# Gated cross attention and six layers on one core: the norm between them placed inside the last turns and the first pass

## What is computed

```python
x = x + jnp.tanh(g_xattn[0]) * _L0_xattn_ref(_layernorm(x), ctx_1024, ctx_1024, ...)
x = x + jnp.tanh(g_ffn[0]) * _L0_ffn_ref(_layernorm(x), ...)
# _L0_ffn_ref:
for i in range(6):
    x = attn_layer(shift_tokens(x), ...) + x
    x = ffn_layer(shift_tokens(x), ...) + x
```

## Time and profile before

| | us |
|---|---|
| median of 3 runs | 1986.11 (1985.73 to 1987.90) |
| profiled execution, its time | 1993.02 |
| its span | 1991.2 |
| PE busy | 1858.3 (93% of the span) |
| DVE busy | 1589.7 (80%) |
| ACT busy | 1045.7 (53%) |
| POOL busy | 903.9 (45%) |
| cross attention, up to the last `x1` update | 0 to 266.3 |
| the norm between, up to the first projection | 266.3 to 290.1 |

### The profile page before, as it was taken

The page is one execution under the profiler, slowest core; times in us unless marked ns, Lnnn a source line. Parts: engine busy times, 40 slices in busy tenths (PEclk is TensorE's granted clock), DMA queues, the critical chain, the costliest instruction groups (busy, mean ns, idle before and its releaser), DMA issues.

```text
span 1991.2 us, 84866 instructions
## 1 busy us (share of the span) xinstructions
PE 1858.3 (93%) x35408; PEld 1303.1 (65%) x35408; DVE 1589.7 (80%) x3092; ACT 1045.7 (53%) x1879; POOL 903.9 (45%) x1231
## 2 busy tenths in 40 slices
PE   6888858899999999999999999999999999999996
PEld 3444424676767777777767677776767676777674
DVE  5565557788988888888888888888889888888883
ACT  2444423455555656555555556565556555465553
POOL 1000015364554646464555546464645555464640
PEclk7898888999999999999999999999999999999997
DMA  2001006556566656566565666565665646564650
GB/s 69 10 7 64 0 3 100 83 80 102 74 122 109 94 82 94 117 95 108 78 104 72 122 109 94 82 93 117 93 110 76 106 71 124 104 95 83 91 91 22
DMA packets 73332, 166.87 MB, mean 84 GB/s; under 512 B 16592, under 2 KB 23504, under 8 KB 72400
## 3 DMA queue, kind: packets, MB, share of 16 engines
q0 software_dynamic: 36864, 100.71, 37.9%
q1 hardware_dynamic: 36432, 65.68, 12.7%
HBM read 20.57 MB, written 1.05 MB: 11 GB/s over the span
## 4 chain that ended last, share of the span: by engine, by line
PE 69%; DVE 9%; issue 7%; DMA 2%; ACT 0%; DVEq 0%; POOL 0%; POOLq 0%; ACTq 0%
PE ps L997 14%; PE ps L1033 8%; PE ps L1087 7%; PE ps L1107 6%; PE ps L1057 6%; PE ps L1141 5%; PE ps L1009 5%; PE ps L1070 4%; PE ps L1100 3%; DVE big L815 3%; PE ps L1131 3%; PE ps L1021 3%; DVE big L825 2%; DMA big<-big 2%; PE ps L1048 2%
## 5 line engine op out<-in xcount | busy, mean ns | idle before, releaser
L477 POOL DMA_DIRECT2D big<-big x768 | 607.0, 1497 | 62.4 <-DVE big L807 43.9
L564 ACT ACTIVATE big<-ps 128x512 f32<-128x512 f32 x384 | 228.4, 595 | 587.6 <-PE ps L997 540.0
L997 PE MATMUL ps<-big,wn_sb 128*128 128x256 f32 x1536 | 411.2, 396 | 17.5 <-issue 14.9
L815 DVE TENSOR_TENSOR big<-big,ps 128x512 f32<-128x512 f32 x384 | 249.6, 680 | 93.2 <-PE ps L1021 82.8
L997 PEld LDWEIGHTS ps<-big,wn_sb 128*128 128x128 f32 x1536 | 275.4, 192 | 69.6 <-issue 16.5
L468 POOL TENSOR_TENSOR big<-big 128x512 f32<-128x512 f32 x96 | 123.4, 1285 | 360.8 <-ACT big L581 360.8
L804 DVE TENSOR_TENSOR big<-ps,tab 128x512 f32<-128x512 f32 x384 | 262.0, 682 | 11.0 <-ACT big L564 10.9
L807 DVE TENSOR_TENSOR big<-ps,tab 128x512 f32<-128x512 f32 x384 | 259.0, 674 | 0.0
L1141 PE MATMUL ps<-big,wo_sb 128*128 128x256 f32 x768 | 214.5, 382 | 0.0
L443 POOL COPY big<-xs 64x256 f32 x144 | 79.2, 550 | 263.5 <-DVE xs L843 257.6
L1033 PE MATMUL ps<-wn_sb,big 128*64 128x512 f32 x768 | 182.0, 611 | 0.7 <-DVE big L807 0.7
(11 more groups left out here) (146 smaller groups left out, 2917.1 us busy)
## 6 DMA issues: line engine op xcount, KB each, us to landing
big<-big POOLq DMA_DIRECT2D x768, 128.0 KB, 5.0
big<-big SPq DMA_DIRECT2D x96, 256.0 KB
big<-big SPq DMA_DIRECT2D x96, 192.0 KB
wn_sb<-in_wn SPq DMA_DIRECT2D x6, 1024.0 KB, 10.0
wn_sb<-in_wn SPq DMA_DIRECT2D x6, 512.0 KB, 6.1
wo_sb<-in_wo SPq DMA_DIRECT2D x6, 512.0 KB, 4.0
w_sb<-in_w SPq DMA_DIRECT2D x6, 341.0 KB, 3.0
w_sb<-in_w SPq DMA_DIRECT2D x6, 192.0 KB, 3.3
```

The lines of the kernel that those rows point to most:

```text
L477: eng.dma_start(rot[to:to + 32, at:at + 4, :], src[32 * r:32 * r + 32], accum_op=ALU.add).then_inc(added[i], 16)
L564: eng.activation(sq[:, two, :], ps[:, i % 2, :].rearrange("p (a t) -> p a t", a=2), ACT.Square).then_inc(sq_d, 1)
L815: eng.tensor_tensor(hat[:, two, :], rot[:, two, :], ps[:, i % 2, :].rearrange("p (a t) -> p a t", a=2), ALU.mult).then_inc(hat_d, 1)
L997: mm = eng.matmul(ps[:, k % 2, a * T:a * T + T], wn_sb[:, u * P:u * P + P], sT, start=True, stop=True)
```

## The change

The norm of chunks 0, 1 and 2 (batches 0 to 5) is done inside turn 8, in the banks 0 and 1. Chunk 3 (batches 6 and 7, whose `x1` is complete only after turn 9) is centred and gets its variance, Ln and Exp behind turn 9, in the banks 4 and 5; its Newton step and product are put on DVE inside pass 0, behind `n`. PE makes the centred x directly, with the matrix `center` (identity minus mean), so the subtraction on DVE goes; Ln takes eps as its bias and the Newton step reads the variance from PSUM with + EPS in the same instruction, so the addition of eps goes. The scratch is three slots in a part of `big` that the cross attention doesn't use. POOL's zeroing moves ahead of its waits, and POOL and PE begin the layers with `nxn` at 3. The diff, cut to its core:

```diff
@@ -167,11 +167,8 @@
-        xc0 = view(CH * CW, CH, CW)
-        sq0 = view(CH * CW, CH, CW)
-        va0 = view(CH * CW, CH, CW)
-        z0 = view(CH * CW, CH, CW)
-        z1 = view(CH * CW, CH, CW)
+        used[0] = 22784
+        sq0, z0, z1 = (view(3 * CW, 3, CW) for _ in range(3))
         assert used[0] <= BIG
@@ -239,8 +236,10 @@
-        nmean, nxc, nsq, nvar, nva, nln, ny, nxn, nt = (
-            sem(n) for n in ("nmean", "nxc", "nsq", "nvar", "nva", "nln", "ny", "nxn", "nt"))
+
+        LN_BANKS = [(0, 1), (0, 1), (0, 1), (4, 5)]
+        nmean, nsq, nvar, nln, ny, nxn, nt = (
+            sem(n) for n in ("nmean", "nsq", "nvar", "nln", "ny", "nxn", "nt"))
@@ -428,13 +427,13 @@
             cross(eng, cross_body)
-            eng.wait_ge(nxn, CH)
-
...
             eng.wait_ge(zero, 7)
+            eng.wait_ge(xres, B + FREE)
+            eng.wait_ge(nxn, CH - 1)
@@ -485,7 +484,18 @@
+            def norm_squares(c):
+                eng.wait_ge(nmean, c + 1)
+                eng.activation(sq0[:, c % 3, :], ps[:, LN_BANKS[c][0], :], ACT.Square).then_inc(nsq, 1)
+
+            def norm_roots(c):
+                eng.wait_ge(nvar, c + 1)
+                eng.activation(z0[:, c % 3, :], ps[:, LN_BANKS[c][1], :], ACT.Ln, bias=part["eps"]).then_inc(nln, 1)
+                eng.wait_ge(nln, c + 1)
+                eng.activation(z0[:, c % 3, :], z0[:, c % 3, :], ACT.Exp, scale=-0.5).then_inc(ny, 1)
+
             def cross_body(b, X1, X2, X3):
+                late = X2 and not X1
                 def exps(first, last):
@@ -502,6 +512,8 @@
                     exps(0, 2)
+                if late:
+                    norm_squares(0)
                 if X1:
@@ -509,6 +521,8 @@
                     exps(2, 4)
+                if late:
+                    norm_roots(0)
                 if X1:
@@ -523,15 +537,24 @@
                     exps(6, 8)
+                if late:
+                    norm_squares(1)
                 masked(0)
...
                     exps(8, 10)
+                if late:
+                    norm_roots(1)
                 masked(1)
...
                     exps(10, 12)
+                if late:
+                    norm_squares(2)
                 masked(2)
...
                     exps(12, 14)
+                if late:
+                    norm_roots(2)
+                if X2:
                     eng.wait_ge(xsc, b * H)
@@ -544,15 +567,8 @@
-            for c in range(CH):
-                eng.wait_ge(nxc, c + 1)
-                eng.activation(sq0[:, c, :], xc0[:, c, :], ACT.Square).then_inc(nsq, 1)
-            for c in range(CH):
-                eng.wait_ge(nva, c + 1)
-                eng.activation(z0[:, c, :], va0[:, c, :], ACT.Ln).then_inc(nln, 1)
-            for c in range(CH):
-                eng.wait_ge(nln, c + 1)
-                eng.activation(z0[:, c, :], z0[:, c, :], ACT.Exp, scale=-0.5).then_inc(ny, 1)
+            norm_squares(CH - 1)
+            norm_roots(CH - 1)
@@ -622,6 +638,17 @@
+            def norm_rows(c):
+                eng.wait_ge(ny, c + 1)
+                eng.scalar_tensor_tensor(z1[:, c % 3, :], z0[:, c % 3, :], -0.5, z0[:, c % 3, :], ALU.mult, ALU.mult).then_inc(nt, 1)
+                eng.wait_ge(nt, 3 * c + 1)
+                eng.scalar_tensor_tensor(z1[:, c % 3, :], ps[:, LN_BANKS[c][1], :], EPS, z1[:, c % 3, :], ALU.add, ALU.mult).then_inc(nt, 1)
+                eng.wait_ge(nt, 3 * c + 2)
+                eng.scalar_tensor_tensor(z1[:, c % 3, :], z1[:, c % 3, :], 1.5, z0[:, c % 3, :], ALU.add, ALU.mult).then_inc(nt, 1)
+                eng.wait_ge(nt, 3 * c + 3)
+                eng.tensor_tensor(xs[:, 2 * c:2 * c + 2, 1:T + 1], ps[:, LN_BANKS[c][0], :].rearrange("p (a t) -> p a t", a=2),
+                                  z1[:, c % 3, :].rearrange("p (a t) -> p a t", a=2), ALU.mult).then_inc(nxn, 1)
+
@@ -668,6 +695,9 @@
                     eng.tensor_tensor(x1b, x1b, xproj, ALU.add).then_inc(xres, 1)
+                if X2 and not X1:
+                    for c in range(CH - 1):
+                        norm_rows(c)
                 if X1:
@@ -691,27 +721,6 @@
-
-            for c in range(CH):
-                eng.wait_ge(nmean, c + 1)
-                eng.tensor_tensor(xc0[:, c, :], x1[:, 2 * c:2 * c + 2, :].rearrange("p a t -> p (a t)"), ps[:, c, :],
-                                  ALU.subtract).then_inc(nxc, 1)
-            for c in range(CH):
-                eng.wait_ge(nvar, c + 1)
-                eng.tensor_scalar(va0[:, c, :], ps[:, 4 + c, :], EPS, None, ALU.add).then_inc(nva, 1)
-            for c in range(CH):
-                eng.wait_ge(ny, c + 1)
-                eng.tensor_tensor(z1[:, c, :], z0[:, c, :], z0[:, c, :], ALU.mult).then_inc(nt, 1)
-            for c in range(CH):
-                eng.wait_ge(nt, c + 1)
-                eng.scalar_tensor_tensor(z1[:, c, :], z1[:, c, :], -0.5, va0[:, c, :], ALU.mult, ALU.mult).then_inc(nt, 1)
-            for c in range(CH):
-                eng.wait_ge(nt, CH + c + 1)
-                eng.scalar_tensor_tensor(z1[:, c, :], z1[:, c, :], 1.5, z0[:, c, :], ALU.add, ALU.mult).then_inc(nt, 1)
-            for c in range(CH):
-                eng.wait_ge(nt, 2 * CH + c + 1)
-                eng.tensor_tensor(xs[:, 2 * c:2 * c + 2, 1:T + 1], xc0[:, c, :].rearrange("p (a t) -> p a t", a=2),
-                                  z1[:, c, :].rearrange("p (a t) -> p a t", a=2), ALU.mult).then_inc(nxn, 1)
@@ -790,6 +799,8 @@
                         eng.tensor_scalar(n_s, ps[:, 2, 0:T], 1e-24, 65536.0, ALU.max, ALU.mult).then_inc(ss_d, 1)
+                        if not Bh:
+                            norm_rows(CH - 1)
                     if kind == "N":
@@ -856,6 +867,17 @@
+            def center(c):
+                eng.wait_ge(xres, 2 * c + 2 + FREE)
+                if 0 < c < CH - 1:
+                    eng.wait_ge(nxn, c)
+                eng.matmul(ps[:, LN_BANKS[c][0], :], part["center"], x1[:, 2 * c:2 * c + 2, :].rearrange("p a t -> p (a t)"),
+                           start=True, stop=True).then_inc(nmean, 1)
+
+            def variance(c):
+                eng.wait_ge(nsq, c + 1)
+                eng.matmul(ps[:, LN_BANKS[c][1], :], mean_w, sq0[:, c % 3, :], start=True, stop=True).then_inc(nvar, 1)
+
@@ -939,14 +961,20 @@
                     tokens()
+                late = X2 and not X1
                 if X2:
                     scores(0)
+                if late:
+                    center(0)
+                if X2:
                     scores(1)
...
                     normed_tokens()
+                if late:
+                    variance(0)
                 if X2:
@@ -961,6 +989,10 @@
                         step(*which)
+                    if late:
+                        for at, do, c in ((0, center, 1), (2, variance, 1), (4, center, 2), (6, variance, 2)):
+                            if at == n:
+                                do(c)
                 if X2:
@@ -974,14 +1006,9 @@
             eng.wait_ge(xres, B + FREE)
-            for c in range(CH):
-                eng.matmul(ps[:, c, :], mean_w, x1[:, 2 * c:2 * c + 2, :].rearrange("p a t -> p (a t)"),
-                           start=True, stop=True).then_inc(nmean, 1)
-            for c in range(CH):
-                eng.wait_ge(nsq, c + 1)
-                eng.matmul(ps[:, 4 + c, :], mean_w, sq0[:, c, :], start=True, stop=True).then_inc(nvar, 1)
-            eng.wait_ge(nxn, CH)
-
+            center(CH - 1)
+            variance(CH - 1)
+            eng.wait_ge(nxn, CH - 1)
```

## The result

The changed kernel takes 1982.39 us, the median of 20 executions (1977.11 to 1993.87); the kernel before, over 20 executions beside it, 1990.02 (1985.73 to 1994.21). The ratio is 0.9964, 95% interval 0.9953 to 0.9975; applied to 1990.02 that is 7.2 us less, between 5.0 and 9.4. The forecast was 9.1 less and 1977.0, range 1972.5 to 1981.5: the sign is right, the size a little too large, and the time lies outside the range. Of the 5.4 us between 1977.0 and 1982.39, 3.9 are the kernel before itself: the three executions from which I counted had a median of 1986.11, the twenty 1990.02.

A forecast was written before the change was run, and what follows sets the result against it. PE, busy 93% of the span, was taken as the bound, with gains only where it stands still. -19.1 + 5.6 + 1.5 + 2.9 = -9.1, from 1986.1 to 1977.0 us, range 1972.5 to 1981.5.

The forecast's parts named there:

- Behind turn 9: From the last x1 update to the first projection: 4.65 us instead of 23.8, so -19.1 us.
- Turn 8, the walk: PE's order in turn 8 with six matmuls put in, including a 2.95 us stall before center(2): +5.6 us.
- `center(0)` falls into the 0.88: nothing: In turn 8, center(0) (0.86 us) fits PE's 0.88 us wait for DVE ahead of the output projection, at no cost.
- The clock: In turn 8, one stretch of about 3.4 us at half clock behind the stall: +1.5 us, ends 0 and +3.4.
- rival E: Turn 8 falls to half clock as a whole: slower by 3.4 us, up to +10 if pass 0 follows; chance 0.04.
- Pass 0: norm_rows(3) between n and c7, d7 delays m3, the values and the heads' norm: +2.9 us.
- The alternative that I named and didn't take: In pass 0, if m3's DMAs were held up by those of m2 rather than their own issue: about +1 us.
- Against the median: Whole kernel: -9.1 carried from the profiled execution to the median of the runs shown, 1986.1 - 9.1 = 1977.0 us.
- B: Clock stays up in turn 8, m3's DMAs hide 2 us in pass 0: -12.6, from -10.5 to -14; chance 0.17.
- C: Two half-clock stretches in turn 8, one over V1 to V3 in pass 0: -5.2, from -7.5 to -4; chance 0.18.
- A: The forecast: turn 8 loses about 7, behind turn 9 wins 19, pass 0 pays 3: -9.1, -7.5 to -10.5; chance 0.53.
- D: Turn 8 pays the whole serial chain of three chunks, 18.3 us: sum about +2, from -4 to +4; chance 0.08.

The follow-up runs named there:

- scores_paired: The changed kernel with center(0) behind scores(1) instead of between scores(0) and scores(1); ratio to the kernel before 0.9943, turns 8 and 9 35.34 us.
- clock_kept: The changed kernel with six extra matmuls of 256 columns, results unread, in the pause ahead of center(2); ratio to the kernel before 0.9947, turns 8 and 9 31.41 us.
- rows3_ahead: The changed kernel with norm_rows(3), DVE's four instructions for the last chunk, ahead of pass 0, behind the tables; ratio to the kernel before 0.9954, turns 8 and 9 31.25 us.
- all_behind: The change's norm, but chunks 0 to 2 behind turn 9 instead of in turn 8, each in its own banks; ratio to the kernel before 0.9990.
- rows3_split: The changed kernel with norm_rows(3) cut in two, first half ahead of pass 0, second ahead of c4; ratio to the kernel before 0.9946, pass 0 26.96 us.
- change_longer: The changed kernel with six extra matmuls of 256 columns in turn 9, during the division; ratio to the kernel before 0.9934.

## Why the prediction was right or wrong

*Behind turn 9* (-19.1): right, -19.3. Centre, square and variance at half clock took 4.51 us where I had 4.65; POOL's shift, the tables and the roots were ready, as said.

*Turn 8, the walk* (+5.6): the mechanism was right, the size too small. That `center(2)` waits for DVE's `xs` of the chunk before, that PE's `weigh` and ACT's exps are queued behind it, and that it is the only such wait: all in the trace, at 2.82 us for 2.95. Wrong was "`center(0)` falls into the 0.88: nothing". L973 began 3.86 us after the first scores instead of 2.80. I had priced a matmul by its own rate, 0.86, from a row of eight equal ones; between others one costs 1.05 (240.06 to 241.11), and it parted two `scores` that run into each other when they are neighbours; scores_paired puts that at 0.7. With 0.2 more for `center(1)` over its 0.84 of cover, the walk should have said 6.9 (31.2 us for turns 8 and 9); clock_kept and rows3_ahead, both at full clock, show 7.1 and 6.95.

*The clock* (+1.5, ends 0 and +3.4): in the profiled execution +3.0, in rows3_ahead 0, in two others some +9. The range of this term was too narrow, and rival E, in part, is no remote case: in two of four executions of this order the first 15.6 us of the turn were at half clock, with PE busy 97% of the slow stretch or more, so the pauses that I gave as its cause aren't the whole cause. What held the clock down there I can't say. Against E I had written that the clock came back within 3.4 us of work "after each of the slow stretches in the trace". The trace of the kernel before says otherwise. Between 17.4 and 41.2 us it holds a slow stretch of 23.8 us, with PE busy 18.89 of them:

```profile
17.40:41.20 23.80, 18.89 (x78) 8.87 (x82) 12.87 (x32) 5.25 (x13) 0.00 (x0) 0.50 0.04 12
```

The same matmuls last as long in the changed kernel (1.18 us for a group of four at L918), though its clock column shows 1.00 for that stretch: a granted clock is to be read together with the lengths of the matmuls. The mean of the four turns is 36.6 us, 12.3 more than before; with -19.3 and +2.1 that is -4.9, the one profiled execution of the change gives -7.2, and the measured -7.2 (5.0 to 9.4 less) has the first at its edge.

*Pass 0* (+2.9): +2.1. "No slack turns up" was wrong. The alternative that I named and didn't take, +1, was the right mechanism: the DMAs of m3 no longer queue behind those of m2, and 1.9 us of wait before H5 went. The half clock over the values, which I had put at 0, took back 1.3 of it. That +2.1 lies near +2.9 is luck, two errors against each other.

*Against the median*: this is the step that failed, the one that put the time outside the range. I wrote that the 6.9 us between the profiled execution and the median of three were "one of the way of running". They were scatter: over 20 executions the kernel before has 1985.73 to 1994.21, and the profiled 1993.02 lies in it. Three executions did not bound its median to better than 4 us, and the range of 9 us had nothing for that. From 1990.0 the same -9.1 gives 1980.9, and the same range 1976.4 to 1985.4, which holds 1982.39. The bounds themselves, -13.6 and -4.6, aren't the ones that their sentence names either: B's middle is -12.6 and C's ends are -7.5 and -4. The change itself was over-rated by 1.9 us: turn 8 with its clock cost 2.9 more than forecast, pass 0 0.8 less, the stretch behind turn 9 0.2 less.

*Rivals.* B fell by its clock half and held by its DMA half. C's two terms both came (two slow stretches, one over the values), with the DMA slack against them. The measured -7.2 lies at the line between A and C. D is refuted by the ratio and by the timeline, where only the third chunk waits. Something of it holds: all_behind shows that the placement in turn 8 is worth little beyond the new arithmetic, much less than it looks.

## What to carry to other kernels

Work moved into a turn that is already a ping-pong of two engines costs what its waits cost, in order, on every engine that it passes: here the same matmuls cost 7 us or 4 at full clock, by whether the one that waits for a buffer stands before or behind the work that doesn't. Place a dependent chain so that each link is asked for one stage later than it can be ready, and cut it into the gaps that the timeline names (pass 0: four instructions at +2.1 us in one place, at nothing in two). When a change is worth 0.4%, compare stretches between fixed events, not spans: turn 8 began between 235.6 and 246.1 us, and from pass 1 to the end it took 1666.1 to 1677.6, with the same work. Even a stretch wants more than one profile: turn 8 of the same order differed by 9 us. And a forecast from a median of three executions carries their scatter, here 4 us.

## What the runs showed of the hardware

The clock stayed at its lower level for 20.5 us while PE was busy 19.95 of them in rows3_split, and as long in change_longer; other executions of the same order left it after 3.4 us. In the kernel before it stayed there for 23.8 us, from 17.4 to 41.2, PE busy 18.89. An idle stretch of 2.82 us was followed by 6.8 us at half clock in the change and by none in rows3_ahead.

Twenty-four PE instructions more, at three places ahead, took 5 to 7.6 us from the first pass through the loop of the layers, which began 70 us or more later (34.1 to 34.6 us for 39.7 to 41.7). The page of each profile counts 23 packets on the queue of instructions (q8), and the pauses are about 2 us each; that each pause waits for such a packet is argued, not shown.
